# Second key sums ahead of the last chunk's product, and sums normalised in quarters with a thin product for queries without keys

## The reference, cut to what matters

```python
x = x + xattn(layernorm(x), ctx, ctx, mask, Wq, bq, Wk, bk, Wv, bv, Wo, bo)
    # q, k, v: projections of width 128, 16 heads of 8
    scores = jnp.einsum('bhqd,bhkd->bhqk', q, k) / sqrt(8)
    scores = jnp.where(mask[:, None, :, :], finfo.min, scores)
    ctx = jnp.einsum('bhqk,bhkd->bhqd', softmax(scores), v); out = ctx @ Wo.T + bo
x = x + ffn(layernorm(x), gate_w, w1, b1, w2, b2)
    # softmax of 8 gate logits, the best two; for each: gelu(x @ w1 + b1) @ w2 + b2, summed by their probability
```

## Time and profile before

| what | value |
|---|---|
| median of 3 runs | 332.46 us (331.86 to 334.14) |
| the profiled execution | 330.95 us |
| its span, first to last instruction | 329.3 us |
| busy share of the span: PE, DVE, ACT, POOL | 81%, 54%, 70%, 24% |
| mean granted clock of TensorE | 0.967 |

### The profile page before, as it was taken

The page is one execution under the profiler, slowest core; times in us unless marked ns, Lnnn a source line. Parts: engine busy times, 40 slices in busy tenths (PEclk is TensorE's granted clock), DMA queues, the critical chain, the costliest instruction groups (busy, mean ns, idle before and its releaser), DMA issues.

```text
span 329.3 us, 6448 instructions
## 1 busy us (share of the span) xinstructions
PE 267.3 (81%) x1941; PEld 134.8 (41%) x1944; DVE 176.7 (54%) x431; ACT 230.0 (70%) x366; POOL 80.5 (24%) x137
## 2 busy tenths in 40 slices
PE   2689978989999989898989898966777577799940
PEld 2455534122121212121222222254666577798940
DVE  4799864354535363535454535476963125677612
ACT  4458856999999999999999999716951212555520
POOL 8891013000000000100010004030387105344430
PEclk9999999999999999999999999999979597999995
DMA  7999580101010101010100101895011521100115
GB/s 214 360 402 404 195 178 6 41 2 40 0 40 12 28 12 28 12 28 14 26 21 19 26 14 28 304 317 89 17 49 51 145 57 35 32 29 30 34 36 187
DMA packets 29011, 29.31 MB, mean 89 GB/s; under 512 B 15341, under 2 KB 22913, under 8 KB 28864
## 3 DMA queue, kind: packets, MB, share of 16 engines
q1 hardware_dynamic: 27536, 26.21, 26.2%
q0 software_dynamic: 1456, 2.86, 2.9%
HBM read 21.62 MB, written 7.45 MB: 88 GB/s over the span
## 4 chain that ended last, share of the span: by engine, by line
PE 45%; ACT 19%; issue 16%; DVE 11%; DMA 3%; another core or an unknown queue 2%; DVEq 2%; ACTq 1%; POOL 0%; POOLq 0%; SPq 0%
PE bank L1385 12%; ACT w2T L1073 10%; PE bank L1367 7%; PE bank L1494 6%; PE bank L1502 3%; PE bank L1235 3%; ACT arenaB L1073 3%; PE bank L1512 2%; PE bank L1196 2%; DVE arenaB L949 1%; PE bank L1261 1%; ACT w1T L1099 1%; ACT w2T L1099 1%; DMA x_sb<-in_x_dram 1%
## 5 line engine op out<-in xcount | busy, mean ns | idle before, releaser
L756 DVE TENSOR_TENSOR arenaA<-bank,arenaA 128x512 f32<-128x512 f32 x80 | 55.2, 691 | 80.0 <-PE bank L1385 80.0
L1073 ACT ACTIVATE arenaB<-bank 128x1024 f32<-128x1024 f32 x80 | 77.5, 1021 | 2.8 <-PE bank L1367 0.7
L1073 ACT ACTIVATE w2T<-bank 128x1024 f32<-128x1024 f32 x80 | 76.6, 1029 | 3.4 <-PE bank L1367 2.9
L1367 PE MATMUL bank<-qS,keys 64*128 64x512 bf16 x328 | 62.7, 386 | 10.7 <-ACT w2T L1073 7.6
L1106 ACT ACTIVATE mask_u<-bank,arenaB 128x128 f32<-128x128 f32 x92 | 26.3, 369 | 46.5 <-PE bank L1494 41.7
L1367 PEld LDWEIGHTS bank<-qS,keys 64*128 64x128 bf16 x328 | 15.5, 92 | 98.0 <-ACT w2T L1073 51.4
L1385 PE MATMUL bank<-arenaB,vcur 128*32 128x512 f32 x320 | 42.6, 604 | 2.8 <-DVE vcur L749 2.6
L1385 PE MATMUL bank<-w2T,vcur 128*32 128x512 f32 x320 | 42.6, 605 | 0.0
L411 POOL CAST keep<-flags 128x1 f32 x12 | 2.3, 189 | 161.1 <-DVE arenaC L649 139.6
L1494 PE MATMUL bank<-arenaB 128*128 128x128 f32 x184 | 28.1, 302 | 10.9 <-DVE arenaB L941 9.9
L1494 PEld LDWEIGHTS bank<-arenaB 128*128 128x128 f32 x184 | 24.7, 209 | 13.2 <-DVE arenaB L941 11.9
(11 more groups left out here) (318 smaller groups left out, 349.0 us busy)
## 6 DMA issues: line engine op xcount, KB each, us to landing
mask_u<-in_L_ffn_w_dram SPq DMA_DIRECT2D x2, 2048.0 KB, 10.5
mask_u<-in_mask_BxSxS_bk_dram SPq DMA_DIRECT2D x6, 560.5 KB, 12.6
ctx_sb<-in_ctx_dram SPq DMA_DIRECT2D x3, 768.0 KB, 13.4
qS<-qparts_dram SPq DMA_DIRECT2D x4, 448.0 KB
mask_u<-in_mask_BxSxS_bk_dram SPq DMA_DIRECT2D x6, 240.0 KB, 10.8
keys_in<-kparts_dram SPq DMA_DIRECT2D x40, 32.0 KB
mask_u<-in_mask_BxSxS_bk_dram SPq DMA_DIRECT2D x1, 1121.0 KB, 7.5
qparts_dram<-arenaA SPq DMA_DIRECT2D x2, 512.0 KB, 8.1
```

The source lines that it names most:

```text
L756: nc.vector.tensor_tensor(a, bank[:, 4 + k % 2, :], a, ALU.add).then_inc(s["ac"], 1)
L1073: nc.scalar.activation(probs[u % 8], bank[:, 2 * (u % 2):2 * (u % 2) + 2, :].rearrange("p a b -> p (a b)"), ACT.Exp, scale=SCALE).then_inc ...
L1367: last = mm(bank[:, 2 * (u % 2) + a, :], keys[rows, g, :], qS[rows, g, cols], start=not hides, stop=True, tile_position=(64 * a, 0))
```

## The change

- **Key sums.** `key_sums(1)` and its waits stand ahead of the last chunk's product instead of behind it, three of the `keep_busy` products around it are gone, and `plan_counts` follows the last chunk but one's squares. ACT no longer writes one bank of zeros (`zero_sums(1, 2)`) in the middle of the chunks; it writes three banks after them instead of two.
- **The ladder behind the plan.** The bound's product stands ahead of the first key product. The first tile's value product has its own place in bank 3 and stands ahead of the mask's turn. The two register loads of PE stand ahead of the second half of `first_keys`. `products(0)` no longer stands behind `hide(1)`.
- **Fill.** The default rows of `xs_dram` (now 8 DMAs for the same 23 row tiles) are sent ahead of the tile loop's key rows instead of behind it, after a loop over the tiles with a partly hidden mask.
- **Normalising.** Quarters of two query tiles instead of halves of four. DVE's term for queries without keys is gone (two operations of 512 elements a half). In its place the flags are turned (L1485 of the new kernel) and multiplied with `uniform`, a 16-row matrix which comes from the mean value and the output weights (L1504, then ACT). That product is a second matmul into the same place for every query tile (L1495).
- **Gate.** The variance step stands after the one-hot sums. Expert weights 0 to 3 are turned ahead of the rank products, and two are copied by ACT ahead of the root.
- **Rows.** The copies of the gate's turned weights (`epi_e`) go from DVE to ACT, and all of `rows[1]` is made after the weights' copies. `FIRST` is 5. `b2_products` stands ahead of `tile_rows(0)`, its addition to `x2` at the end. `stage` of the first two tiles that are read back is done within the loop over the first five. The table of experts by tile is made after two `places`.

```diff
+
+U_BANKS, AT_BANKS = (0, 2, 5, 0), (7, 2, 3, 5)
+W_BANKS = (0, 1, 4, 6)
...
-FIRST = 4
...
+FIRST = 5
...
-XS_CUTS = [(FIRST, 6), (0, FIRST), (6, 12), (12, 18), (18, NT)]
+XS_CUTS = [(FIRST, 8), (0, FIRST), (8, 13), (13, 18), (18, NT)]
...
-            with sp.Fori(1, n + 1) as i:
-                key_rows(i, 1, s["kch"], s["kw"], s["kr"], s["kc"])
+            with sp.If(partial):
+                with sp.Fori(1, partial + 1) as i:
+                    key_rows(i, 1, s["kch"], s["kw"], s["kr"], s["kc"])
+
+            sp.wait_ge(s["fill"], 2)
+            for b, tiles in enumerate(SPARE):
+                sp.dma_start(xs_dram.rearrange("(j s) c -> s j c", s=P)[:, tiles[0]:tiles[-1] + 1:3, :],
+                             fill[:, b:b + 1, :].broadcast_to([P, len(tiles), ROW])).then_inc(s["xs_fill"], 16)
+            with sp.If(n - partial):
+                with sp.Fori(partial + 1, n + 1) as i:
+                    key_rows(i, 1, s["kch"], s["kw"], s["kr"], s["kc"])
 
...
+            def normalise(qd):
+
+                dve.wait_ge(s["u_ps"], qd + 1)
+                b = U_BANKS[qd]
+                U = bank[:, b:b + 2, :].rearrange("p t (h c) -> p t h c", c=32)
+                c0 = 4 * qd
...
+                nc.vector.tensor_scalar(flag, U[:, :, :, HD], 0.0, None, ALU.is_equal).then_inc(s["u_dve"], 1)
...
+                nc.vector.tensor_tensor(weight, flag, U[:, :, :, HD], ALU.add).then_inc(s["u_dve"], 1)
+                dve.wait_ge(s["u_dve"], c0 + 2)
+                nc.vector.reciprocal(inv, weight).then_inc(s["u_dve"], 1)
                 dve.wait_ge(s["u_dve"], c0 + 3)
-                nc.vector.tensor_tensor(cq, tmp, U[:, :, 0:HD], ALU.add)
-                nc.vector.reciprocal(inv, weight).then_inc(s["u_dve"], 1)
-                dve.wait_ge(s["u_dve"], c0 + 4)
-                nc.vector.tensor_tensor(cq, cq, over(inv), ALU.mult).then_inc(s["u_dve"], 1)
-            dve.wait_ge(s["gxr"], 5)
-            for hf in range(2):
...
+            def joined(qd):
+                dve.wait_ge(s["at_ps"], qd + 1)
+                ts = slice(2 * qd, 2 * qd + 2)
+                o = bank[:, AT_BANKS[qd], :].rearrange("p (u c) -> p u c", c=256)
                 nc.vector.tensor_tensor(lgx[:, ts, :], o[:, :, D:D + XE], gx[:, ts, :], ALU.add).then_inc(s["x2s"], 1)
                 nc.vector.tensor_tensor(x2[:, ts, :], x_sb[:, ts, :], o[:, :, 0:D], ALU.add).then_inc(s["x2s"], 1)
+
+            for qd in range(4):
+                normalise(qd)
+            dve.wait_ge(s["gxr"], 5)
+            for qd in range(4):
+                joined(qd)
...
@@ -958,18 +980,15 @@
             slot_rows(0)
             stage(1)
             slot_rows(1)
-            for j in range(3, FIRST):
-                places(j)
+            places(2)
             for j in range(FIRST):
+                if j + 3 < FIRST:
+                    places(j + 3)
+                stage(j + 2)
                 if j + 2 < FIRST:
-                    stage(j + 2)
                     slot_rows(j + 2)
                 dve.wait_ge(s["yps"], j + 1)
                 nc.vector.tensor_copy(y_first[:, j, :], bank[:, 4 + j % 2, 0:P]).then_inc(s["yacc"], 1)
-            dve.wait_ge(s["b2ps"], 1)
-            nc.vector.tensor_tensor(x2, x2, bank[:, 6:8, :].rearrange("p a (t d) -> p (a t) d", d=D), ALU.add).then_inc(s["b2ps"], 1)
-            stage(FIRST)
-            stage(FIRST + 1)
             slot_rows(FIRST)
             slot_rows(FIRST + 1)
...
+            dve.wait_ge(s["b2ps"], 1)
+            nc.vector.tensor_tensor(x2, x2, bank[:, 6:8, :].rearrange("p a (t d) -> p (a t) d", d=D), ALU.add).then_inc(s["b2ps"], 1)
...
-                if c == 11:
-                    act.wait_ge(s["q_sb"], 4)
-                    zero_sums(1, 2)
...
+            act.wait_ge(s["q_sb"], 4)
             act.wait_ge(s["qw"], 16 * len(Q_RUNS))
             act.wait_ge(s["qn_ps"], 1)
-            zero_sums(2, 4).then_inc(s["ac"], 1)
+            zero_sums(1, 4).then_inc(s["ac"], 1)
...
+            def context_turned(qd):
+                act.wait_ge(s["cq_ps"], qd + 1)
+                nc.scalar.activation(turned[:, qd, :], bank[:, 4, :], ACT.Copy).then_inc(s["cq_sb"], 1)
+
+            act.wait_ge(s["cs_ps"], 3)
+            nc.scalar.activation(uniform, bank[0:H, 4, 0:D + XE], ACT.Copy, scale=1.0 / S2).then_inc(s["cs_sb"], 1)
+            for qd in range(4):
+                context_turned(qd)
             for t in range(QT):
-                act.wait_ge(s["x2s"], 2 * (t // 4) + 2)
+                act.wait_ge(s["x2s"], 2 * (t // 2) + 2)
                 nc.scalar.activation(squared[:, t, :], x2[:, t, :], ACT.Square, bias=lgx[:, t, E:XE], accum_out=ln[:, 0, t:t + 1]).then_inc(s["gtexp"], 1)
+            expert_weights(0, 2)
             act.wait_ge(s["sqrt2"], 1)
             nc.scalar.activation(ln[:, 1, :], ln[:, 0, :], ACT.Sqrt).then_inc(s["gtexp"], 1)
...
-                nc.scalar.activation(dst, bank[:, 4 + k % 4, :].rearrange("p (a b) -> p a b", a=FT), ACT.Copy).then_inc(s["wtb_sb"], 1)
+            expert_weights(2, 16)
+            for k in range(2):
+                act.wait_ge(s["gT_ps"], k + 1)
+                nc.scalar.activation(epi_e[:, 512 * k:512 * k + 512], bank[0:E, 5 + 2 * k, :], ACT.Copy).then_inc(s["gT_sb"], 1)
+            act.wait_ge(s["sqrt2"], 7)
+            for t in range(QT):
+                nc.scalar.activation(rows[1][:, t, 0:D], x2[:, t, :], ACT.Identity, scale=ln[:, 3, t:t + 1], bias=ln[:, 4, t:t + 1]).then_inc(s["cq_sb"], 1)
...
-                if c == CHUNKS + 1:
+                if c == CHUNKS:
                     pe.wait_ge(s["kb_sb"], 1)
                     pe.wait_ge(s["bd"], 1)
                     pe.wait_ge(s["pick"], 1)
-                    keep_busy(bank[:, 2, :], 2)
                     key_sums(1)
-                    keep_busy(bank[:, 7, :], 1)
+                if c == CHUNKS + 1:
                     plan_counts()
...
             pe.wait_ge(s["plan_ready"], 1)
             tile0 = pe.value_load(plan[0:1, 0:1], min_val=0, max_val=T - 1)
+            pe.wait_ge(s["bd"], 6)
+            mm(bank[0:1, 2, 0:H], norms[:, 2:3], ident[0:H, 0:H], start=True, stop=True).then_inc(s["bd_ps"], 1)
             pe.wait_ge(s["cc_sb"], CHUNKS)
             mm(b6[:, P:2 * P], wk_turned[:, :], ctx_sb[:, bass.ds(tile0, 1), :].rearrange("p a k -> p (a k)"), start=True, stop=True).then_inc(s["k_first"], 1)
-            pe.wait_ge(s["bd"], 6)
-            mm(bank[0:1, 2, 0:H], norms[:, 2:3], ident[0:H, 0:H], start=True, stop=True).then_inc(s["bd_ps"], 1)
...
-            first_keys(4, G)
             pe.wait_ge(s["gen_ready"], 1)
             partial = pe.value_load(plan[0:1, 66:67], min_val=0, max_val=T)
             general = pe.value_load(plan[0:1, 65:66], min_val=0, max_val=1)
-            pe.wait_ge(s["cb"], 1)
-            project_values().then_inc(s["kv"], 1)
+            first_keys(4, G)
...
             pe.wait_ge(s["mc"], 1)
             hide(0, 0)
-            pe.wait_ge(s["cs_sb"], 3)
-            hide(1, 0)
             pe.wait_ge(s["qr"], 64)
             pe.wait_ge(s["qzero"], 2)
             pe.wait_ge(s["kc"], 1)
             products(0, True)
+            pe.wait_ge(s["cs_sb"], 3)
+            pe.wait_ge(s["vn"], 1)
+            hide(1, 0)
             products(1, True)
...
-            for hf in range(2):
-                pe.wait_ge(s["u_dve"], 5 * hf + 5)
-                for t in range(4 * hf, 4 * hf + 4):
-                    last = nc.tensor.transpose(bank[:, t // 4, (t % 4) * P:(t % 4 + 1) * P], ctxq[:, t, :], ident[:, :])
+            def context_turn(qd):
+
+                if qd:
+                    pe.wait_ge(s["cq_sb"], qd)
+                else:
+                    pe.wait_ge(s["cs_sb"], 6)
+                pe.wait_ge(s["u_dve"], 4 * qd + 4)
+                for t in range(2):
+                    nc.tensor.transpose(bank[0:H, 4, (2 + t) * P:(3 + t) * P], after[:, 5120 + 32 * qd + H * t:5120 + 32 * qd + H * (t + 1)], ident[:, :])
+                for t in range(2):
+                    last = nc.tensor.transpose(bank[:, 4, t * P:(t + 1) * P], ctxq[:, 2 * qd + t, :], ident[:, :])
                 last.then_inc(s["cq_ps"], 1)
-                pe.wait_ge(s["cq_sb"], hf + 1)
-                for t in range(4 * hf, 4 * hf + 4):
-                    last = mm(bank[:, 2 + t // 2, 256 * (t % 2):256 * (t % 2) + D + XE], ctxqT[:, t * P:(t + 1) * P], wo_x, start=True, stop=True)
+
+            def projected(qd):
+                pe.wait_ge(s["cq_sb"], qd + 1)
+                for t in range(2):
+                    to = bank[:, AT_BANKS[qd], 256 * t:256 * t + D + XE]
+                    mm(to, turned[:, qd, t * P:(t + 1) * P], wo_x, start=True, stop=False)
+                    last = mm(to, turned[0:H, qd, (2 + t) * P:(3 + t) * P], uniform, start=False, stop=True)
...
-            keep_busy(b6, 12)
-            pe.wait_ge(s["x2s"], 4)
+
+            pe.wait_ge(s["ac"], n * 8 + 2)
+            pe.wait_ge(s["vc"], n + 1)
```

(16 more changed lines are left out.)

156 lines of the change are left out of this document (71 added, 85 removed).

## The result

| | median, us | runs | profiled span |
|---|---|---|---|
| kernel before | 332.16 | 331.14 to 334.14, 4 runs | 329.3 |
| changed kernel | 341.98 | 340.97 to 343.17, 4 runs | 338.9 |

The ratio is 1.029, with a 95% interval of 1.023 to 1.035. The forecast was 329.3, the range 319.5 to 335. The two profiled executions, cut at the same places, give the account. "x2 complete" is the end of DVE's last sum with x.

What follows compares the result with a forecast made beforehand. ACT bounds the tile loop, PE the stretch 276.70 to 316.00, a ladder of hand-overs what lies between. Sum: -1.5 + 1.1 + 2.7 - 5.4 = -3.1, a median of 329.3 us; range 319.5 to 335, likeliest case 326.5 to 332.

Steps and rivals of the forecast that it cites:

- The key sums: Start: sums in the last product's place and no zeros amid the chunks gain 1.3 us (1.0 to 2.2).
- the ladder: From the plan to the first exponential: reordered products and register loads gain 0.2 us (-0.2 to 0.6).
- The fill: Tile loop: default rows queued ahead delay the second tile's key rows, plus 1.1 us once (0 to 3).
- The quarters: Normalising after the loop: four rungs of about 2.4 us replace two of 2.54, plus 2.5 (1.2 to 3.6).
- 8 records: Product step in each quarter's rung: as many records as a half's product, which took 1.20 us.
- The clock: Rival: standing still in the quarter rungs lowers the clock to 0.5; 335.7 us, 337.6 with the fill's 3; chance 0.13.
- the rule that transposes don't engage the full clock: Quarter rungs: by it they would run at 1.2 GHz, 335.7 us; the forecast followed the trace instead, 329.3.
- the same waits at half the number left the clock at 1.00: Argument against a clock fall in the quarter rungs, from the kernel before's two halves.
- Behind the scatters: From the scatters to the streamed tiles: the release moves by +2.3, later steps together give -5.4 us.
- the fifth tile's 3.9: Direct tiles: one more tile's gathering and two layers, 32 records at 0.122 each, plus 3.9 us.
- b2's 2.05: Direct tiles: `b2_products` moves in front of the release, ahead of the first gathered rows, minus 2.05 us.
- The first rival: Behind the scatters: PE's late announcements vanish and direct tiles run through; 322 us (318.5 to 326), chance 0.22.

Runs made afterwards that it cites:

- x1: The changed kernel with the 8 fill DMAs back behind the tile loop's key rows and weight loads; 339.06 us (335.5 to 341.8).
- y2: The kernel before with only the fill DMAs moved ahead of the tile loop's key rows; 323.65 us against 320.17.
- x5: The changed kernel with a second product of 128 rows in place of the 16-row thin one; 321.32 us, 7.5 below the changed kernel.
- x3: The changed kernel with two banks for the turned quarters, each turned before the quarter ahead is multiplied; 335.16 us.
- x4: The changed kernel without the flags' turns and the thin products, ACT copying 256 columns instead of 512; 316.96 us against the kernel before's 320.17.
- z1: The changed kernel with the fill behind the loop, two banks for turned quarters, and 2 wide matmuls ahead of each product; 316.65 us against the kernel before's 320.17.
- z2: The changed kernel with the fill behind the loop, no thin product, and the term for queries without keys back on DVE; 311.65 us against the kernel before's 320.19.
- y3: The kernel before with both start parts, b2's sum into x2 behind all tiles, and early stages of two streamed tiles; 315.76 us against 320.17.

## Why the prediction was wrong

**The key sums and the ladder: right in kind, too small.** I took 1.3 for the sums, near the low end of 1.0 to 2.2, on the ground that DVE's joining of the mask isn't sped up. It did not need to be: the mask was there at 40.1, and both gains that I had named, the sums' place and the 1.05 of zeros in the middle of the chunks, came nearly in full (2.13 of 2.2 at the flags). Another 1.0 came from the ladder, which I had put at 0.2. Measured -3.13, outside my bounds of 0.8 to 2.5.

**The fill: right mechanism, a quarter of its size.** x1 and y2 show the stall to be the fill's alone. The term was 1.1 and measured 4.84, beyond the bound of 3. Of the difference 1.6 is the start: the copy fell due at 65.8, since the loop began earlier than forecast. Another 1.7 is the write of the key rows, which I had landing one us behind the fill, at 63, and which could be read at 64.73; the last 0.4 is the reads. What I mis-sized was a small transfer behind a full queue: 6.4 us from issue to landing, in y2 as well (60.19 to 66.62), against 2.26.

**The quarters: the step that failed.** The step was "8 records", priced at 1.20 as before, "since every query tile gets a thin second product". The count was right and the price wrong: the matmuls alternate between 128 and 16 rows, and then all records start 0.21 apart (0.43 for two), where records of 128 rows start 0.117 apart (0.23 for two, x5). That makes a rung of 3.00, where the forecast had 2.4 and x5 with 128 rows has 2.33: 2.4 us over four rungs. I had also written a low end for the case that the 16-row products take half; they took longer. The other 3.9 of the 6.4 that were missing is the clock: the rungs take 3.00, 3.50, 4.72 and 4.72.

**The clock: a rival that named the wrong cause.** I gave it 0.13 and tied it to PE standing still in the rungs and to the removed `keep_busy` matmuls. The result is on its side (slower, the clock at 0.5 from 225 to 239, x2 and the weights' turns late), though over its 335.7 and its 337.6. But x3 has hardly a gap and the low clock, while x4 and x5 have the gaps, lack the twelve `keep_busy` too, and have the full clock. What tells them apart is the thin product. Of the rule that transposes don't engage the full clock, which I weighed by the Trainium skill's page "TensorE: Matmul & The Clock Gate", Part 4: x5 has every turn of the changed kernel at a clock of 1.00, so the runs speak against it as the cause here. (I named the stretch 218.40 to 227.60 for the turns of the sums; they ended at 218.03, ahead of it, also at 1.00. And the kernel before has four low stretches, not three: at 242.6, 256.2, 273.3 and 321.1. Nothing in the sum hangs on either.) My argument "the same waits at half the number left the clock at 1.00" looked at waits, and the new thing in the rung was the kind of product.

**Behind the scatters: steps right, the setting wrong.** I forecast -5.4 there and measured -1.41. In the groups in which PE's results were announced in time the new late phase does gain: 80.2 us for the repeated changed kernel, 80.1 for z1, 79.0 for x4, 78.8 for x5 and 77.6 for z2, against 83.1 for the old one in y2, 3 to 5.5 less. y3 shows 3.3 of it for the late sum and the stages. In the first pair of profiles most of that is missing, and the late announcements stand in two places where it could go: the release comes with the last scatter in both kernels, and again at 290, where 5 dense result scatters were out, ACT waits, and so does the row ahead of PE's next product:

```profile
290.09 1.14 ACT L1136 ACTIVATE mask_u<-bank,arenaB 128x128 f32<-128x128 f32 x4 [3.02 <-remote]
290.12 0.29 DVE L963 COPY arenaB<-bank 128x128 f32<-128x128 f32 x1 [1.25 <-remote]
```

From the release to the first streamed pair both kernels take 14.9 us. I had counted the fifth tile's 3.9 and b2's 2.05 against one another as if all else were equal at the release; but the kernel before had gone through two gelus and a second layer by then (252.54, 255.45, 253.74), and the changed one had done two first layers and no gelu.

**The first rival, late announcements that don't come back,** was right about something else: they come and go from group to group with the same kernel. They are very likely why the kernel before takes 320 or 332: y2 has its late phase, with the announcements in time, and takes 83.1 in it where the first profile takes 94.74; those 11.6 are nearly the 12.0 between 332.2 and 320.2. (Of the kernel before at 320 there is no profile.) The difference between the kernels is nearly the same either way, 8.6 and 9.8.

**What stays open.** Why PE's announcements are late in some groups and not in others: no kernel here controls it. The three groups of experiments ran on three different chips, so it may be the chip; but on the first of them the kernel before took 323 and 330 in turn, so it isn't the chip alone. Which property of the thin product brings the clock down: its 16 rows, the zeros in it, or the slower starts; a thin product of other data, or a wide one of zeros, was not run. And whether the missing `keep_busy` matmuls cause the low clock that the repeated changed kernel had at its start.

## What to carry to other kernels

Price a small matmul in a chain by its neighbours, not by its size: a 16-row product between 128-row ones costs more than a full one in its place, and may take the clock with it, while the same sum on DVE cost 1.0 us over four quarters (z2 against x4). A bulk write placed "where nobody waits for it" must not stand on the queue ahead of a small transfer whose reader has 4 us of slack. And when a profile shows waits that no busy engine explains, run the unchanged kernel several times on its own before counting on them.

## What the hardware showed that I had not expected

- Starts of the records of f32 matmuls of 137 columns: 0.117 us apart in a row of 128-row ones (two records in 0.23, x5), 0.21 where 128 and 16 rows alternate (two in 0.43, changed kernel).
- A granted clock of 0.50 with PE busy for 4.00 of 4.00 us (x3). A busy share of 1 in this view is no guard.
- PE's matmul results known to ACT up to 10.8 us after the matmul's end while scatters were out (changed kernel, a first layer that ended at about 258.0 and was seen at 268.8), and in the second and third groups not at all, with the same scatters at the same pace (20.9 us from the first start to the last in the changed kernel, 20.7 to 21.5 in those groups).
